# One tile of a fused adaLN, attention and expert kernel: expert rows by two products with a split table, scores and first layer in one product, that layer transposed for two tiles at once, and a new order of work

## The reference, cut to what matters

```python
cluster_scores = xf @ cluster_sigs.T          # 8 columns
tile_scores    = xf @ sigs.T                  # 64 columns
# calibrate both, best cluster, best of its 8 tiles -> tile_idx
h    = gelu(xf @ compress_w1 + compress_b1)   # 256 -> 64, the first layer
comp = tanh(h @ compress_w2 + compress_b2)    # 64 -> 2
hh   = relu(comp @ spline_w1[tile_idx] + spline_b1[tile_idx])
mag  = hh @ spline_w2[tile_idx] + spline_b2[tile_idx]
y    = layernorm(xf + mag * directions[tile_idx] * output_scale)
```

## Time and profile before

| | |
|---|---|
| median of 3 runs | 1919.03 us (1913.91 to 1920.64) |
| the profiled execution | 1920.77 us |
| its span | 1919.0 us |
| mean granted TensorE clock | 0.977 |
| PE busy | 96% |
| DVE busy | 85% |
| ACT busy | 64% |
| POOL busy | 56% |
| DMA | 43 GB/s mean |

### The profile page before, as it was taken

The page is one execution under the profiler, slowest core; times in us unless marked ns, Lnnn a source line. Parts: engine busy times, 40 slices in busy tenths (PEclk is TensorE's granted clock), DMA queues, the critical chain, the costliest instruction groups (busy, mean ns, idle before and its releaser), DMA issues.

```text
span 1919.0 us, 63488 instructions
## 1 busy us (share of the span) xinstructions
PE 1836.4 (96%) x25286; PEld 1489.1 (78%) x25286; DVE 1629.5 (85%) x4120; ACT 1237.6 (64%) x2514; POOL 1065.0 (56%) x775
## 2 busy tenths in 40 slices
PE   4899999999999999999999999999999999999974
PEld 3688888878888887887888888788888878878762
DVE  5577888888888899888889888888988988898765
ACT  2566676666667666666766666666666676666642
POOL 0455565565565566556556655655655565565522
PEclk7899999999999999999999999999999999999985
DMA  4011122122112112112211211221121121122121
GB/s 145 9 26 37 41 46 46 40 42 44 39 44 44 37 42 44 44 38 46 42 38 44 44 44 38 41 45 40 44 44 39 40 44 44 38 47 43 44 48 28
DMA packets 337972, 83.09 MB, mean 43 GB/s; under 512 B 277007, under 2 KB 336879, under 8 KB 337903
## 3 DMA queue, kind: packets, MB, share of 16 engines
q1 hardware_dynamic: 337902, 82.12, 19.6%
HBM read 48.51 MB, written 33.55 MB: 43 GB/s over the span
## 4 chain that ended last, share of the span: by engine, by line
PE 93%; DVE 4%; POOL 1%; ACT 1%; issue 1%; SPq 0%; DMA 0%; POOLq 0%; ACTq 0%; DVEq 0%
PE pa L439 29%; PE ps L518 6%; PE pa L446 6%; PE pb L418 6%; PE ps L505 6%; PE ps L469 5%; PE ps L476 4%; PE pc L652 3%; PE pc L538 3%; PE pa L418 3%; PE ps L562 3%; PE pb L425 3%; PE pb L610 3%; PE pb L513 2%; PE ps L520 2%; PE pb L430 2%
## 5 line engine op out<-in xcount | busy, mean ns | idle before, releaser
L1106 POOL TENSOR_TENSOR yve<-ymv,eps 128x1 f32<-128x1 f32 x64 | 12.1, 190 | 547.3 <-DVE ymv L1007 547.3
L439 PE MATMUL pa<-wq,xnTs 128*128 128x512 f32 x768 | 213.4, 414 | 0.0
L439 PE MATMUL pa<-wv,y 128*128 128x512 f32 x768 | 210.4, 410 | 1.9 <-ACT kn L782 0.3
L439 PE MATMUL pa<-wk,y 128*128 128x512 f32 x768 | 211.8, 411 | 0.0
L1098 POOL TENSOR_TENSOR rn<-nrg,mhalf 128x16 f32<-128x16 f32 x64 | 203.4, 3177 | 4.2 <-DVE nrg L1055 3.7
L1086 POOL TENSOR_TENSOR rn<-nrg,mhalf 128x16 f32<-128x16 f32 x64 | 186.6, 2915 | 17.7 <-DVE nrg L1033 11.6
L439 PEld LDWEIGHTS pa<-wv,y 128*128 128x128 f32 x768 | 134.8, 188 | 32.3 <-issue 5.4
L1091 POOL TENSOR_TENSOR bd<-vm,pick 128x1024 f32<-128x1024 f32 x64 | 121.9, 1905 | 65.3 <-PE pc L652 61.5
L439 PEld LDWEIGHTS pa<-wq,xnTs 128*128 128x128 f32 x768 | 137.4, 192 | 24.9 <-ACT kcat L736 0.3
L439 PEld LDWEIGHTS pa<-wk,y 128*128 128x128 f32 x768 | 134.7, 188 | 27.8
L1103 POOL TENSOR_TENSOR pr<-pr,rden 128x1056 f32<-128x1056 f32 x64 | 135.9, 2123 | 2.9 <-DVE rden L927 2.9
(11 more groups left out here) (222 smaller groups left out, 5206.1 us busy)
## 6 DMA issues: line engine op xcount, KB each, us to landing
xT<-in_xT SPq DMA_DIRECT2D x64, 128.0 KB, 2.4
x<-in_x SPq DMA_DIRECT2D x64, 128.0 KB, 2.1
x1d<-x SPq DMA_DIRECT2D x64, 128.0 KB, 1.7
kxdr<-kxn SPq DMA_DIRECT2D x64, 128.0 KB, 1.7
vm<-kxdr SPq DMA_DIRECT2D x128, 64.0 KB, 2.8
odr<-o SPq DMA_DIRECT2D x256, 32.0 KB, 2.0
on<-odr SPq DMA_DIRECT2D x64, 128.0 KB, 2.1
xb<-x1d SPq DMA_DIRECT2D x64, 128.0 KB, 2.1
```

The costliest lines, as they stand in the source:

```text
L439: last = mm(bank, part(lhs(a_, k)), part(rhs(b_, k)), start=(n == 0), stop=(n == 3 * CK - 1))
```

## The change

In words, part by part:

1. The expert rows: `gath` is split at setup into a float32r high part and the rest (`gath2`, 322 columns each, the last one zero). The fetch is two float32r products that add up, in place of one float32 product. `ohT` is written as float32r.
2. The scores and the first layer are one pair of products of 136 columns with all of `wsc`, in place of a pair of 72 columns and a pair with 64 rows and 128 columns. The first layer so comes out untransposed; ScalarE copies it to `hidn`, one half a tile, and one transpose a pair of tiles turns both halves at once. Gelu, with the bias, reads that transpose from PSUM. 
3. The second layer is one product a pair, with a 128 by 4 weight matrix with zero blocks, and its bias goes into two Tanh instructions.
4. The order of every engine's `step` is rewritten, the place where a step begins is moved, and the stages run to tile `i - 10`; one more step is written out at the end.

The core of the diff:

```diff
-        LOADS = {"cond_in": 8, "small_in": 7, "wk_in": 1, "wv_in": 1, "wq_in": 1, "late_in": 7}
+        LOADS = {"cond_in": 8, "small_in": 7, "wk_in": 1, "wv_in": 1, "wq_in": 1, "late_in": 8}
...
-            for i in range(last, T + 9):
+            for i in range(last, T + 10):
...
-                    for k in range(CK):
-                        mm(pb[:, C:C + NS], zT[:, k, :], wsc[:, k, 0:NS],
-                           start=(k == 0), stop=(k == CK - 1), skip_group_check=True)
-                    for k in range(CK):
-                        last = mm(pb[0:CH, C + P:C + 2 * P], wsc[:, k, NS:NS + CH], zT[:, k, :],
-                                  start=(k == 0), stop=(k == CK - 1), skip_group_check=True)
+                    for k in range(CK):
+                        last = mm(pb[:, C:C + NS + CH], zT[:, k, :], wsc[:, k, :],
+                                  start=(k == 0), stop=(k == CK - 1), skip_group_check=True)
...
-                    mm(pb[:, 0:GATH], ohT[:, :], gath[:, :], start=True, stop=True).then_inc(S("gathered"), 1)
+                    for a in range(2):
+                        last = mm(pb[:, 0:GATH + 1], part(ohT[:, :]), part(gath2[:, a, :]), start=(a == 0), stop=(a == 1))
+                    last.then_inc(S("gathered"), 1)
...
+                if live(i, 8):
+                    if p == 1:
+                        nc.tensor.transpose(pb[:, C:C + P], hidn[:, :, :].rearrange("p u h -> p (u h)"), ident[:, :])\
+                            .then_inc(S("hT_mm"), 2)
...
-                    if p == 0:
-                        for u in range(2):
-                            mm(pb[:, C + P + 2 * u:C + P + 2 * u + 2], hT[:, u, :], w2b[:, :], start=True, stop=True)
+                    if 1 - p == 0:
+                        mm(pb[:, C + P:C + P + 4], hT[:, :], w2b[:, :], start=True, stop=True)
...
-                    fn(hT[0:CH, 1 - p, :], pb[0:CH, C + P:C + 2 * P], ACT.Identity, bias=b1[:, :]).then_inc(S("hidden"), 1)
-                    wait(act, "hidden", t7)
-                    if 1 - p == 1:
-                        fn(hT[0:CH, :, :], hT[0:CH, :, :], ACT.Gelu).then_inc(S("gelu_done"), 2)
+                    fn(hidn[:, p, :], pb[:, C + NS:C + NS + CH], ACT.Copy).then_inc(S("hidden"), 1)
...
+                    if p == 1:
+                        fn(hT[:, :], pb[:, C:C + P], ACT.Gelu, bias=b1[:, :]).then_inc(S("gelu_done"), 2)
...
+            fn(part(gath2[:, 0, 0:GATH]), gath[:, :], ACT.Copy).then_inc(S("gath_high"), 1)
...
+            v.tensor_tensor(part(gath2[:, 1, 0:GATH]), gath[:, :], gath2[:, 0, 0:GATH], ALU.subtract)
...
                 if live(i, 0):
+                    if live(i, 2):
+                        wait(dve, "v1_mm", t2)
                     wait(dve, "yT_mm", i)
                     modulate(yT, two(pa[:, 2, :], 0), dem[:, 0, :, :], i).then_inc(S("y_dem"), 1)
```

More of the change, by code:

```diff
@@ L335, in step @@
             def step(i, p):
[L336 to L347, removed]
+                t2, t4, t5, t6, t7, t10 = i - 2, i - 4, i - 5, i - 6, i - 7, i - 10
                 if live(i, 0):
@@ L489, in step @@
-                if live(i, 5):
[L490 to L499, removed]
@@ L515, in step @@
-                    last.then_inc(S("score_mm"), 1)
-                if live(i, 4):
+                    wait(pe, "o2_done", t7)
+                if live(i, 6):
+                    wait_dma(pe, "v2_in", t6, p, 2)
+                    for h in range(2):
+                        last = nc.tensor.transpose(pc[:, h * P:(h + 1) * P], vm[:, p, h * P:(h + 1) * P], ident[:, :])
+                    last.then_inc(S("mix_kT"), 1)
+                if live(i, 3):
+                    wait(pe, "qT1_done", t3)
+                    four(pa[:, 1, :], kn, 4).then_inc(S("kT1_mm"), 1)
@@ L617, in step @@
+                if live(i, 6):
+                    wait(pe, "a_done", t6)
                     for h in range(2):
@@ new lines, in step @@
+                if live(i, 10):
+                    wait(act, "ohT_mm", t10)
+                    if p == 0:
+                        for o in range(2):
+                            fn(comp[:, :, o], pb[:, C + P:C + P + 4].rearrange("p (u o) -> p o u", o=2)[:, o, :], ACT.Tanh,
+                               bias=b2[:, o:o + 1])
+                    fn(part(ohT[:, :]), pb[0:NT, C:C + P], ACT.Copy).then_inc(S("ohT_done"), 1)
+                if live(i, 3):
+                    wait(act, "qT0_mm", t3)
+                    if live(i, 4):
+                        wait(act, "sim_mm", t4)
+                    fn(qT[:, 0:4, :].rearrange("p r t -> p (r t)"), pa[:, 0, :], ACT.Identity,
+                       bias=0.0, scale=qks[:, 0:1]).then_inc(S("qT0_done"), 1)
@@ new lines, in step @@
+                if live(i, 6):
+                    wait(act, "mix_kT", t6)
+                    for g in range(QG):
+                        last = fn(kbd[:, g, :], pc[:, 0:2 * P], ACT.Identity, bias=0.0, scale=pick4[:, g:g + 1])
+                    last
+                if live(i, 3):
+                    wait(act, "kT1_mm", t3)
+                    fn(kcat[:, 4:8, :, NN:J], pa[:, 1, :].rearrange("p (r s l) -> p r s l", s=BT, l=L),
+                       ACT.Identity, bias=0.0, scale=qks[:, 1:2]).then_inc(S("kcat1_done"), 1)
```

740 lines of the change are left out of this document (375 added, 365 removed).

## The result

The changed kernel takes 2197.38 us (median of 4 runs, 2190.63 to 2203.04) against 1918.44 before: a ratio of 1.1456, 95% interval 1.1417 to 1.1495. The forecast was 1859 us, faster; the time lies far outside its range and beyond its slower rival, 2027.

What follows compares the result with a forecast made beforehand. TensorE, 96% busy, was taken as the bound. Terms saving 1.22 us a tile, less 0.2 of stalls, gave 1.0 net; 60 tiles took 1920.8 to 1860.8, and 1.7 off for the median gave 1859 us, range 1836 to 1908.

Steps and rivals of the forecast that it cites:

- slower rival: GpSimd's `spread` also precedes the last of `yT`: `pr_add` 3.0 us late, 1.8 beyond the gain; 2027 us; chance 0.10.
- What bounds the kernel: Whole kernel: TensorE, 96% busy, sets the 28.08 us tile; VectorE, at 24.9 us, is the one to watch.
- the terms on PE: TensorE's savings per tile: 0.70 + 0.22 + 0.085 - 0.055 + 0.19 + 0.08 = 1.22 us, leaving 26.86 us.
- the 0.19: Extra time of the output-product half behind the small first-layer tiles, 1.92 against 1.73 us, counted as saved.
- The return from small tiles: Products behind small tiles take 0.19 us longer; with the mix directly behind the last scores, paid once, not twice.
- the direct step: From last scores to mix, 64x64 to 64x32 pieces: a drain here would leave nearly no gain instead of 0.19 us.
- the stalls of 0.2: TensorE stalls left by the new order: 0.2 us a tile, bounds 0 and 1.22, leaving net 1.0 us.
- What hides the rest: Walk through the new order's waits: `pr_add` done 3.8 us after `v1_mm`, 1.6 early for the output product at 5.4.
- The rivals: Smaller TensorE savings, 1883 us, 0.18; three GpSimd products ahead of `yT`, 1895 to 1918, 0.10; slower, 0.10.
- The ends: Fill and drain outside the full stretch: taken as 0 us change, between -6 and +10.

Runs made afterwards that it cites:

- the version with both cures: Changed kernel, GpSimd waiting for `yT` ahead of its four products, plus 93 or 10 tiny TensorE transposes ahead of the loop: 1860.51 or 1857.59 us.
- the best version: Changed kernel, GpSimd waiting for `yT` ahead of its key product, plus 10 tiny TensorE transposes ahead of the loop: 1857.59 us, ratio 0.9675.
- the full yield: Changed kernel with 93 tiny TensorE transposes ahead of the loop, GpSimd waiting for `yT` ahead of all four products: 1860.51 us, ratio 0.9702.
- a pad of 100: Kernel before, with only 100 tiny transposes (200 TensorE instructions) added ahead of the loop: 2076.60 us, ratio 1.0827.
- the yield: Changed kernel with one more wait: GpSimd starts its row of four products only when VectorE has finished `yT`; alone 2007.92 us, ratio 1.0468.

## Why the prediction was wrong, step by step

**What bounds the kernel, and the terms on PE: right.** The chain of the version with both cures:

```profile
...
908.91 1.73 PE ps L524 x8
...
911.59 0.47 PE pb L533 x4
...
927.10 0.22 PE pc L629 x2
...
929.59 1.03 PE pc L664 x64
...
930.68 0.65 PE pa L452 x4
931.33 0.49 PE pb L494 x2
...
932.63 1.73 PE ps L507 x8
...
```

The joined product takes 0.47 us, as forecast; the fetch 0.49 (forecast 0.46 to 0.55); both halves of the output product 1.73, so the 0.19 did belong to what stood ahead. The return from small tiles is paid once: 0.65 for four transposes behind 664 against 0.44 elsewhere, and the direct step from the last scores to 664 costs nothing that the rows show (0.26 and 1.03 us, as in the earlier trace rows). PE alone was put at 26.86 us a tile and the net pace at 27.1; it is 26.80, so the stalls of 0.2 were too many: 3.48 us in 56 tiles, 0.06. With both causes taken away the time is 1857.6 to 1860.5, against 1859. That the two agree so closely is partly luck. From the first to the last of the 64 instructions of line 563 (568 with both cures) it took 1745.0 us before and takes 1669.3 now, 75.7 less where the forecast had 60; what lies outside them takes 12.8 us more, where the forecast had 0 and +10 as its bound.

**What hides the rest: this step failed,** in its DVE half. "DVE makes `yT` behind `v1_mm`: ... it is done at 1.8, and then adds the bias". That took undisturbed durations for instructions beside four GpSimd products. The PE half was right: 505 was put 5.4 after `v1_mm`, and with the cures 507 starts 932.63 - 927.10 = 5.53 after it (629 is the first behind `v1_mm`). Undisturbed, the DVE half is right as well, `yT` 2.1 and `pr_add` 3.9 after `v1_mm` (forecast 1.8 and 3.8):

```profile
...
927.90 0.48 DVE L1076 TENSOR_SCALAR yT<-yT,cols 128x128 f32<-128x128 f32 x2
...
928.88 0.29 DVE L1083 TENSOR_SCALAR yT<-yT 128x256 f32<-128x256 f32 x1
929.64 1.12 DVE L921 TENSOR_TENSOR pr<-ps,alibi 128x924 f32<-128x924 f32 x1 [0.47 <-PE ps L475]
...
```

**The rival "slower" was the mechanism,** and its condition held: `spread` did come ahead of the last of `yT`. It had `pr_add`, which 505 waits for, at 8.4 after `v1_mm`; it is done at 8.3, and 505 starts at 8.4. I gave it 0.10 because `spread` waits for the mix of its own step, "when `yT` should be through". But the two engines take turns, so `yT` was still at 1078 when the mix ended. The rivals had been set apart by how many products win; what matters is that each instruction of the block waits for one.

**Its price was too low.** 505 was to be 3.0 us late a tile, and is 8.36 - 5.53 = 2.8; the waiting is 139.6 / 56 = 2.5 us a tile. But that PE then runs below full clock was in no term, though the earlier trace rows show 0.76 in the drain, where PE waits. PE's longer busy time, most of it the clock, is another 136.8 / 56 = 2.4 us a tile.

**The loop's turn was in no term at all.** The prediction costed the order on each engine and not the program as a thing to be fetched. Nothing in the trace of before warns of it, since that kernel has no hole. It is worth 2197.4 - 2128.9 = 68 us with the port stall in place, and 2007.9 - 1857.6 = 150 without.

**The ends, at 0, and the new order:** the same parts in the old order and without holes take 1886.4, so the new order is worth 29 us of the 62 that the best version gains, its longer ends included: in the old order what lies outside line 563's instructions is 4 us shorter than before, and in the new order 12.8 longer.

What stays open: what the hidden part in front of the program is, and whether it is the number of blocks touched or the place of the branch in its block (0.10 to 0.18 with holes, 0.25 and more without) that decides. The loops have nearly one length, so these runs cannot part the two. The double holes, and the second part of the hole in the changed kernel, behind its branch, fit a loop that begins some dozen instructions ahead of an edge: by the table those loops start at 26.95 and 23.96, and the two with single holes at 26.88 and 27.82. No run was made to test that.

## What to carry to other kernels

When a reorder puts VectorE's SBUF-to-SBUF instructions beside GpSimd's large ones, cost the block as if each waits for a whole GpSimd product, and let the engine with time to spare yield: one semaphore wait was worth 189 to 271 us here. A wait on a TensorE that is otherwise full can cost more than it lasts. Here two waits a step, of 1.6 and 0.9 us, cost about twice their length, since the clock fell behind them; one wait of 0.85 us a step left the mean clock at 0.971, and 53.6 us more of waiting (for `pr` and `yT`) then made the span 73.8 us longer than with the full yield. When a loop's body changes in size, or anything ahead of it does, look at the instruction queue's packets, and at how long the loop's branch takes, before blaming the edit; a few idle instructions ahead of the loop tell within one run whether its place matters.

## What the runs showed that was not expected

- 20 instructions that do nothing, ahead of TensorE's loop, took 68 and 150 us off the time; 200 of them ahead of the unchanged kernel's loop added 160.
- A turn with a hole brings 9 instruction packets and costs 4.6 us (mean of 24, the kernel before with a pad of 100) to 7.9 us (mean of 15, the changed kernel). It lowers the clock for the work behind it: 1.53 us instead of 0.89 for four products in two passes.
- In the changed kernel VectorE's tensor-scalars and GpSimd's products alternate one by one: 1.27 us is the mean of a tensor-scalar on 128 elements a partition in the changed kernel, 0.28 with the yield. GpSimd pays in turn when it comes second: `spread` takes 2.91 us in one step of the version with both cures (2.56 on average) and 1.94 in the changed kernel (1.93).
